# A Trainium2 kernel of four chained residual layers: the odd batch of an adapter moved to the last slot but one, and the split of work around a mixing step changed

## Chip, cores and metric

The kernel runs on one core of one Trainium2 chip. The metric is the time of one execution on the device in microseconds (us). Before the change three runs gave 390.32, 390.70 and 393.04 us, median 390.70.

## What is computed

`x` has 32 batches of 64 rows by 1024 columns, in float32. Four residual layers follow one another; each batch picks its weights by an index:

```python
x = x + einsum('bct,bcd->bdt', x, L0_weights[i0])          # 64x64 mix of the rows, i0 in 0..15
x = x + einsum('bct,bcd->bdt', x, L1_weights[i0])          # a second 64x64 mix, same index
x = x + x @ W.T + 0.5 * (x @ lora_A[i1]) @ lora_B_w.T      # 1024x1024 for all, plus low rank
x = x + x @ L3_weight[i2].T                                # 1024x1024, one of 8 "adapters"
```

The two row mixes act on rows and the two others on columns, so the kernel does the column layers first and mixes rows at the end: for each batch it multiplies a combined 64x64 matrix (layers 0 and 1) with the result of layers 2 and 3.

## The kernel before

**Stage one (to about 186 us)** is layer 2. Products are split in a high and a low part (`fp32r`), three matmuls of 128x128 by 128x512 each, in a scheme with fewer block products (names `P1`, `C11`, `P6`, `C22` and so on). ScalarE (ACT) makes the high part, VectorE (DVE) the low part, SyncE (SP) issues the loads.

DVE also computes a **plan** there, in tiny steps (`plan_steps`, a generator that `take(n)` advances by n pieces): batches of the same adapter are put in pairs, two to a **slot**; an adapter with an odd number of batches has one slot with a single batch. `place` is the position of a batch in this order (twice the adapter's first slot, plus the batch's rank within its adapter). Adapters stand in falling order of their number of slots. Every engine reads the plan's words at run time and branches on them. With these inputs there are 17 slots, 0 to 16. From the counts of matmuls in the trace, slot 4 (the last of the first adapter, of five slots) and slot 16 (the last of all, of an adapter with two slots) hold a single batch.

**Stage two (from about 186 us)** is layer 3, slot by slot. A slot has 8 tiles (k = 0 to 7) of adapter weights. TensorE (PE) does for each tile six matmuls for a pair (`PAIR`, three passes by two halves of 512 columns) or four for a single batch (`ALONE`, two passes by two), line 1469. Written by slot i, the order on PE is (`slot_head`, `slot_tail`):

- tiles 0 to 3 of slot i
- `mix` of slot i-1 (line 1489, four matmuls): the row mix; it needs `r_hi` and `r_lo` of slot i-1
- tiles 4 to 7 of slot i

While PE does the first tiles of slot i, ACT copies the finished rows of slot i-1 as the high part (`rows_hi`, line 750, two instructions), and DVE takes the low part (`rows_lo`, line 1236, two). After `mix`, ACT (`mixed_cols`, line 759) and DVE (`mixed_sum`, line 1247) bring the result to SBUF, and SP stores it. DVE's order in its step i is: `rows_lo` of slot i-1; then, if slot i is the first or the last of an adapter, the low part of four tiles of the next adapter (`adapter_lo`, line 1219); then `mixed_sum` of slot i-1. GpSimd (POOL) makes the low part of the next slot's x (line 467) and the mixing matrices (lines 481 and 483).

**The last slot** is cut by columns (`last_slot`, `columns`): part 0 is columns 0 to 511, part 1 is 512 to 767, part 2 is 768 to 1023, line 1554, all 8 tiles each. Before: part 0, `mix` of the slot ahead (15), part 1, `mix_last` of part 0 (line 1504), six tiles of part 2, `mix_last` of part 1, the other two tiles, six matmuls on no data (line 1308), `mix_last` of part 2. ACT copies each part for `mix_last` to `last_row` (line 815); `last_row` shares memory with the rows of slot 15, which `mix` reads, so this copy waits for `mix`. DVE brings out parts 0 and 1 (line 1282), ACT part 2 (line 831). SP stores slot 15 and then parts 0 and 1 (line 389); ACT issues the store of part 2 (line 833).

Of the kernel before, what the change touches and what calls it, by code (L numbers as in the profile page):

```python
# [13 lines left out]
P = 128  # L14
# [53 lines left out]
def build(nc, xt, indices, w0t, w1, wt, lora_a, lora_b, w3t, plan_c, eye_c, out):  # L68
# [3 lines left out]
    def sb(name, shape, dtype, offset=None):  # L72
        size = 4 * int(np.prod(shape[1:]))
        if offset is None:
            offset = at[0]
            at[0] += (size + 31) // 32 * 32
        return nc.alloc_sbuf_tensor_at(name, shape, dtype, offset=offset)
# [15 lines left out]
    cells = sb("cells", [B, 800], F32)  # L93

    last_mix = sb("last_mix", [P, P], F32, offset=cells_at)
    last_row = sb("last_row", [P, D], F32, offset=aT_at + 4 * KT * CT)
    asked = sb("asked", [B, B], I32)


# [60 lines left out]
    def acc(i):  # L160
        return ps[(1, 3)[i % 2]]
# [7 lines left out]

    def end_acc(p, part):  # L170

        return (acc(p)[:, 0, :], acc(1 - p)[:, 1, 0:256], acc(p)[:, 1, 256:512])[part]

    def end_ps(p, part):

        return (acc(1 - p)[:, 0, :], acc(p)[:, 0, 0:256], acc(1 - p)[:, 1, 0:256])[part]


    events = []
# [22 lines left out]
    def s(name):  # L202
        if name not in sem:
            sem[name] = nc.alloc_semaphore(name)
        return sem[name]
# [64 lines left out]
    def within(eng, value, lo, hi):  # L270
        return nc.s_assert_within(eng.snap(value), lo, hi)
# [5 lines left out]
    with nc.Block() as block:  # L277
# [278 lines left out]
        def _(act):  # L556
# [255 lines left out]
            def last_rows(p, part):  # L812

                act.wait_ge(s("end_left"), part + 1)
                act.activation(last_row[:, END_COLS[part]], end_acc(p, part), ACT.Copy).then_inc(s("end_rows"), 1)

            def last(p):

                act.wait_ge(s("steps"), end_steps)
                act.wait_ge(s("mixed"), end_mixed - 1)  # L820
                rows_hi(1 - p)

                act.wait_ge(s("mixed"), end_mixed)
                last_rows(p, 0)
                act.wait_ge(s(f"stored{1 - p}"), end_stored + 32 * (p - 1))
                mixed_cols(1 - p, ahead)
                last_rows(p, 1)
                last_rows(p, 2)
                act.wait_ge(s(f"stored{p}"), end_stored)
                act.wait_ge(s("end_mixed"), 3)  # L830
                act.activation(stage[:, p, END_COLS[2]], end_ps(p, 2), ACT.Copy).then_inc(s("end_out2"), 1)
                act.wait_ge(s("end_out2"), 1)
                act.dma_start(out_part(end_row, 2), stage[0:T, p, END_COLS[2]]).then_inc(s("end"), 16)

            earlier = None
            for i in range(ENDS):
                earlier, word = step(i, earlier, word)
                if i == LOOK:
                    end_mixed, half, end_word, ahead = end_slot(act, n_slots)
                    odd, end_row = act.snap(end_mixed & 1), batches(end_word)[0]  # L840
                    end_steps = within(act, end_mixed * KT + BEFORE3, KT * ENDS, KT * SLOTS + BEFORE3)
                    end_stored = within(act, half * 32, 32 * (ENDS // 2), 16 * SLOTS)
            with contextlib.ExitStack() as nested:
                for i in range(ENDS, SLOTS - 1):
                    nested.enter_context(act.If(n_slots > i + 1))
                    earlier, word = step(i, earlier, word)
# [7 lines left out]
        def _(dve):  # L854
# [121 lines left out]
            def plan_steps():  # L976
# [23 lines left out]
                def stt(dst, a, k, b, op1, op2):  # L1000
                    after()
                    dve.scalar_tensor_tensor(dst, a, k, b, op1, op2).then_inc(s("chain"), 1)
# [48 lines left out]
                tt(last, first, half, ALU.add)  # L1051
                ts(last, last, -1.0, ALU.add)

                rank, place, wide, places = cell(1), cell(1), cell(B), cell(B)
                stt(row, a, a_own, tri, ALU.is_equal, ALU.mult)
                total(rank, row)
# [1 line left out]
                stt(row[:, 0:NA], e, a_own, first, ALU.is_equal, ALU.mult)  # L1058
                total(place, row[:, 0:NA])
                stt(place, place, 2.0, rank, ALU.mult, ALU.add)  # L1060
                copy(wide, place.to_broadcast([B, B]))
                turned(places, wide)
                yield
# [61 lines left out]
            def take(n=None):  # L1125
                for _ in itertools.islice(making, n):
                    pass
# [63 lines left out]
            t2(1)  # L1191
            x_los(7, stg)
            x_los(8, keep)
            take()
            t4(1)
            x_los(9)
            s1()
# [3 lines left out]
            x_los(11)  # L1201
            x_los(12, stg)
            s4()
            low_parts(2)
            w_los(6, raw_of(w_slot(6)))
            c22(0)
# [95 lines left out]
        def _(pe):  # L1302
# [171 lines left out]

            PAIR, ALONE = ((0, 0), (0, 1), (P, 0)), ((T, 0), (T, 1))

            def slot_part(i, mine, tiles):

                with pe.If(mine[2] < 1):
                    products(i, mine, PAIR, tiles)  # L1480
                with pe.Else():

                    products(i, mine, ALONE, tiles)

            def mix(p, single):

# [39 lines left out]
            def slot_head(i, mine):  # L1526
                if i >= LOOK:
                    next(looking, None)
                slot_ready(i)
                slot_part(i, mine, (0, HALF))  # L1530
                following = slot_record(i + 1) if i < SLOTS - 2 else None
                return following

            def slot_tail(i, earlier, mine):
                if i:
                    pe.wait_ge(s("st"), 4 * i)
                    pe.wait_ge(s("r_lo"), 2 * i)
                    if i > 1:
                        pe.wait_ge(s("staged"), 2 * (i - 1))
                    else:  # L1540
                        pe.wait_ge(s("low_sum"), CH)
                    mix((i - 1) % 2, earlier)
                slot_part(i, mine, (HALF, KT))

            def end_products(p, passes, part, tiles=(0, KT)):

# [13 lines left out]
            def last_slot(p):  # L1560

                def columns(passes):
                    end_products(p, passes, 0)
                    pe.wait_ge(s("st"), end_st)
                    pe.wait_ge(s("r_lo"), end_r_lo)
                    pe.wait_ge(s("staged"), end_r_lo - 2)
                    mix(1 - p, ahead_record[2])

                    end_products(p, passes, 1)
                    mix_last(p, 0)  # L1570
                    end_products(p, passes, 2, (0, END_AT))
                    mix_last(p, 1)
                    end_products(p, passes, 2, (END_AT, KT))


                pe.wait_ge(s("st"), end_st - 4)
                pe.wait_ge(s("r_lo"), end_r_lo - 2)
                pe.wait_ge(s("staged"), end_r_lo - 4)
                mix(p, two_ahead)
                slot_part(3 - p, ahead_record, (HALF, KT))  # L1580
                pe.wait_ge(s("s_lo"), end_r_lo + 4)
                with pe.If(end_record[2] < 1):
                    columns(PAIR)
                with pe.Else():
                    columns(ALONE)
                warm(BRIDGE, acc(1 - p)[:, 1, 256:512])
                mix_last(p, 2)

            pe.wait_ge(s("plan"), 1)
# [51 lines left out]
```

## Time and profile before

| | us |
|---|---|
| median of three runs | 390.70 |
| the profiled execution, as timed | 391.91 |
| its span, first to last instruction | 390.0 |
| PE busy (share) | 378.8 (97%) |
| DVE / ACT / POOL busy | 268.8 / 223.6 / 120.9 |

Times in the profile's rows count from the start of the span. The difference of 1.9 us between the timed execution and its span lies around the span.

### The profile page before, as it was taken

To read this page: it belongs to the slowest core of one execution; us is meant where nothing else is said; L and a number is where in the kernel's file an instruction comes from. 1 tells how busy PE (TensorE), PEld (TensorE's weight loads), DVE (VectorE), ACT (ScalarE), POOL (GpSimd) and SP (SyncE) were. 2 spreads that over 40 slices of the span, in tenths; PEclk is the share of its full clock that TensorE was granted. 3 is DMA by queue.
4 is the path that set the end of the run, shared out by engine and by line. 5 is a ranking of instruction groups with operands and counts; after the bars stand their busy time and mean duration, and the time that the engine had idled before them with its cause. 6 is when DMAs were issued, how large, how long until landed. Compare 5 with 4: busy or idle time off the path is not lost.

```text
span 390.0 us, 7688 instructions
## 1 busy us (share of the span) xinstructions
PE 378.8 (97%) x1760; PEld 314.4 (81%) x1761; DVE 268.8 (69%) x292; ACT 223.6 (57%) x297; POOL 120.9 (31%) x161
## 2 busy tenths in 40 slices
PE   7999999999999999999999999899999999999795
PEld 7888888888888888888888887688888888888574
DVE  3696978856856968456977549952699546899443
ACT  3668658497143784253493449554677357777332
POOL 0000140100003000025864517763258434486300
PEclk9999999999999999999999999999999999999998
DMA  7984904640358485405627224732276322862223
GB/s 245 401 296 163 373 4 134 247 158 4 107 203 289 155 299 196 153 2 216 197 79 217 58 56 145 269 105 58 56 238 202 106 56 57 271 212 63 60 61 86
DMA packets 24187, 61.39 MB, mean 157 GB/s; under 512 B 1906, under 2 KB 2098, under 8 KB 24114
## 3 DMA queue, kind: packets, MB, share of 16 engines
q1 hardware_dynamic: 23792, 60.37, 45.9%
q8 instruction: 30, 0.49, 0.5%
q14 instruction: 43, 0.35, 0.3%
q10 hardware_dynamic: 322, 0.18, 0.2%
HBM read 52.15 MB, written 8.39 MB: 155 GB/s over the span
## 4 chain that ended last, share of the span: by engine, by line
PE 90%; issue 2%; DVE 2%; DMA 1%; DVEq 1%; ACT 1%; POOL 1%; SPq 0%; POOLq 0%; ACTq 0%
PE ps L1469 42%; PE ps L1336 12%; PE ps L1338 12%; PE ps L1337 12%; PE ps L1363 4%; PE ps L1489 4%; PE ps L1554 2%; PE ps L1375 2%; DMA ring_f<-xt 1%; DVE ring L878 1%; DVEq L1146 1%; PE ps L1504 0%; POOL aT L467 0%; ACT ring L568 0%; ACT aT L750 0%
## 5 line engine op out<-in xcount | busy, mean ns | idle before, releaser
L1469 PE MATMUL ps<-ring,aT 128*128 x752 | 173.7, 390 | 0.1
L1469 PEld LDWEIGHTS ps<-ring,aT 128*128 128x128 f32 x752 | 140.9, 188 | 30.3 <-issue 1.2
L1336 PE MATMUL ps<-ring 128*128 128x512 f32 x208 | 81.1, 390 | 0.1
L1337 PE MATMUL ps<-ring 128*128 128x512 f32 x208 | 81.0, 389 | 0.0
L1338 PE MATMUL ps<-ring 128*128 128x512 f32 x208 | 80.9, 389 | 0.0
L467 POOL TENSOR_TENSOR aT<-xT,aT 128x512 fp32r<-128x512 f32 (+1 forms) x36 | 56.4, 1588 | 49.9 <-ACT aT L744 44.6
L1219 DVE TENSOR_TENSOR ring<-raw,ring 128x1024 f32 (+1 forms) x40 | 64.1, 1660 | 5.1 <-ACT ring L730 5.0
L750 ACT ACTIVATE aT<-ps 64x1024 fp32r<-64x1024 f32 x32 | 32.7, 1020 | 48.0 <-PE ps L1469 47.5
L1247 DVE TENSOR_TENSOR stage<-ps,stage 64x1024 f32<-64x1024 f32 x30 | 36.7, 1222 | 31.8 <-ACT stage L759 31.1
L1236 DVE TENSOR_TENSOR aT<-ps,aT 64x1024 fp32r<-64x1024 f32 x32 | 39.1, 1222 | 22.6 <-ACT aT L750 21.9
L1336 PEld LDWEIGHTS ps<-ring 128*128 128x128 f32 x208 | 39.0, 188 | 8.4 <-issue 0.5
L759 ACT ACTIVATE stage<-ps 64x1024 f32<-64x1024 f32 x30 | 30.5, 1017 | 26.5 <-PE ps L1489 26.1
L1338 PEld LDWEIGHTS ps<-ring 128*128 128x128 f32 x208 | 39.0, 188 | 8.2
L1337 PEld LDWEIGHTS ps<-ring 128*128 128x128 f32 x208 | 39.1, 188 | 8.0
L730 ACT ACTIVATE ring<-raw 128x1024 f32 (+1 forms) x40 | 39.5, 1048 | 7.4 <-POOL raw L459 5.0
L617 ACT ACTIVATE xT<-ps 128x512 f32<-128x512 f32 x40 | 22.3, 591 | 19.5 <-PE ps L1338 19.2
L459 POOL TENSOR_TENSOR raw<-raw,eye 128x128 f32<-128x128 f32 x40 | 20.2, 515 | 25.6 <-DMA raw<-w3t 23.6
L878 DVE TENSOR_TENSOR ring<-ring_f,ring 128x1024 fp32r<-128x1024 f32 (+1 forms) x20 | 21.6, 1115 | 7.6 <-ACT ring L568 7.5
L506 POOL TENSOR_TENSOR ring_f<-ring_f,eye 128x128 f32<-128x128 f32 x8 | 5.5, 715 | 65.2 <-DVE ring_f L943 50.7
L744 ACT ACTIVATE aT<-xT 128x512 fp32r (+1 forms) x36 | 19.9, 600 | 3.3 <-DVE xT L954 3.0
L568 ACT ACTIVATE ring<-ring_f 128x1024 fp32r<-128x1024 f32 (+1 forms) x20 | 18.4, 963 | 5.2 <-DVE ring_f L912 3.1
L1489 PE MATMUL ps<-aT,st 128*128 128x512 f32 x64 | 17.6, 396 | 3.7 <-POOL st L483 2.2
(93 smaller groups left out, 330.2 us busy)
## 6 DMA issues: line engine op xcount, KB each, us to landing
raw<-w3t SPq DMA_DIRECT2D x40, 512.0 KB, 4.3
ring_f<-xt SPq DMA_DIRECT2D x8, 1024.0 KB, 8.4
raw<-xt SPq DMA_DIRECT2D x8, 1024.0 KB, 5.0
out<-stage SPq DMA_DIRECT2D x30, 256.0 KB, 3.2
ring_f<-wt SPq DMA_DIRECT2D x4, 1024.0 KB, 7.3
xT<-xt SPq DMA_DIRECT2D x3, 1024.0 KB, 10.9
xT<-wt SPq DMA_DIRECT2D x2, 1024.0 KB, 15.8
ring_f<-wt SPq DMA_DIRECT2D x4, 256.0 KB, 5.9
```

The costliest lines, as they stand in the source:

```text
L467: pool.tensor_tensor(x3_split(i, ks, P + h * T, T), xT[:, ks, bass.ds(which[h] * T, T)], as_f32(x3_split(i, ks, h * T, T)), ALU.subtract). ...
L730: act.activation(dst, adapter_raw(t), ACT.Copy).then_inc(s("w_hi"), 1)
L750: act.activation(r_tile(h)[own, :], acc(p)[own, :, :].rearrange("p a n -> p (a n)"), ACT.Copy)\
L759: act.activation(stage[own, p, :], mixed_ps[h][other, :, :].rearrange("p a n -> p (a n)"), ACT.Copy)\
L1219: dve.tensor_tensor(in_two(unit_of(t, 1)), adapter_raw(t), as_f32(in_two(unit_of(t, 0))), ALU.subtract)\
L1236: dve.tensor_tensor(r_tile(h)[other, :], acc(p)[own, :, :].rearrange("p a n -> p (a n)"), as_f32(r_tile(h)[own, :]), ALU.subtract).then_in ...
L1247: dve.tensor_tensor(dst, mixed_ps[h][own, :, :].rearrange("p a n -> p (a n)"), dst, ALU.add)\
L1336: pe.matmul(dst, hi_of(qw)[:, k, cs], hi_of(qx)[:, k, :], start=start and k == 0, stop=False, skip_group_check=True)
L1337: pe.matmul(dst, hi_of(qw)[:, k, cs], lo_of(qx)[:, k, :], start=False, stop=False, skip_group_check=True)
L1338: last = pe.matmul(dst, lo_of(qw)[:, k, cs], hi_of(qx)[:, k, :], start=False, stop=stop and k == HALF - 1, skip_group_check=True)
L1469: last = pe.matmul(acc(i)[:, n, :], x3_split(i, k, start, P), ring[:, bass.ds(off + (part * D + n * 512), 512)], start=(k == 0 and j == 0) ...
L1489: last = pe.matmul(dst[:, n, :], st[:, p, h, :], r_tile(h)[:, 512 * n:512 * (n + 1)], start=start, stop=stop)
```

## The change

Five edits:

1. **Plan.** Three more cells: `moved` marks adapters with at least three slots; for one with an odd count it becomes the rank 2·half-3, else a rank that no batch reaches. Batches from this rank on are placed one position later. The single batch thus takes the last slot but one, and the last two batches are a pair. For the first adapter (nine batches, five slots) slot 3 now holds the single batch and slot 4 a pair. The adapter of slots 15 and 16 has only two slots and stays as it is.
2. **Tiles ahead of mixing.** A single batch's slot does five tiles ahead of `mix` and three behind, a pair's four and four as before.
3. **Place of the plan's steps on DVE.** What was one run of steps (`take()`) is now six pieces (`take(6)`) there and the rest behind `s4()`.
4. **The last slot.** Parts 0 and 1 now stand ahead of `mix` of slot 15. The accumulators and result places of part 1 and 2 are exchanged to fit.
5. **`last_row`** lies in `raw`, the adapters' load buffer, so ACT copies parts 0 and 1 ahead of the wait for `mix`; it waits for `w_lo` of the last adapter's tiles first.

```diff
-    last_row = sb("last_row", [P, D], F32, offset=aT_at + 4 * KT * CT)
+    last_row = raw[:, 0, :]
...
-        return (acc(p)[:, 0, :], acc(1 - p)[:, 1, 0:256], acc(p)[:, 1, 256:512])[part]
+        return (acc(p)[:, 0, :], acc(p)[:, 1, 0:256], acc(1 - p)[:, 1, 256:512])[part]
...
-        return (acc(1 - p)[:, 0, :], acc(p)[:, 0, 0:256], acc(1 - p)[:, 1, 0:256])[part]
+        return (acc(1 - p)[:, 0, :], acc(p)[:, 0, 0:256], acc(p)[:, 1, 0:256])[part]
...
+                act.wait_ge(s("w_lo"), end_adapter)
+                last_rows(p, 0)
+                last_rows(p, 1)
                 act.wait_ge(s("mixed"), end_mixed)
-                last_rows(p, 0)
                 act.wait_ge(s(f"stored{1 - p}"), end_stored + 32 * (p - 1))
                 mixed_cols(1 - p, ahead)
-                last_rows(p, 1)
                 last_rows(p, 2)
...
+                moved, odd, start = cell(NA), cell(NA), cell(1)
+                ts(moved, half, 3.0, ALU.is_ge)
+                stt(odd, half, 2.0, cnt, ALU.mult, ALU.subtract)
+                tt(odd, odd, moved, ALU.mult)
+                ts(moved, half, 2.0, ALU.mult, float(2 * B - 3), ALU.add)
+                stt(moved, odd, float(-2 * B), moved, ALU.mult, ALU.add)
+                yield
...
+                stt(row[:, 0:NA], e, a_own, moved, ALU.is_equal, ALU.mult)
+                total(start, row[:, 0:NA])
+                ts(rank, rank, start, ALU.is_ge, place, ALU.add)
+                copy(place, rank)
...
             x_los(8, keep)
-            take()
+            take(6)
             t4(1)
...
             s4()
+            take()
             low_parts(2)
...
-            def slot_part(i, mine, tiles):
+            def slot_part(i, mine, second):
+                def tiles(front):
+                    return (front, KT) if second else (0, front)
                 with pe.If(mine[2] < 1):
-                    products(i, mine, PAIR, tiles)
+                    products(i, mine, PAIR, tiles(HALF))
                 with pe.Else():
-                    products(i, mine, ALONE, tiles)
+                    products(i, mine, ALONE, tiles(HALF + 1))
...
                     end_products(p, passes, 0)
+                    end_products(p, passes, 1)
                     pe.wait_ge(s("st"), end_st)
                     pe.wait_ge(s("r_lo"), end_r_lo)
                     pe.wait_ge(s("staged"), end_r_lo - 2)
                     mix(1 - p, ahead_record[2])
-                    end_products(p, passes, 1)
                     mix_last(p, 0)
```

How it moves instructions. First DVE in stage one, between the low parts of `x_los(8)` (the first row) and those of `t4(1)` and `s1()`. Before, the plan's tail and its end stand here (line 1122 writes the last word; 912 is `t4`, 943 is `s1`):

```order
L1002 SCALAR_TENSOR_TENSOR cells<-cells 32x1 x6
L998 TENSOR_SCALAR cells<-cells 32x3 x3
L1010 CAST cells<-cells 32x3
...
L1122 CAST plan<-cells 1x1
L912 TENSOR_TENSOR ring_f<-ring_f,raw 128x2048
L878 TENSOR_TENSOR ring<-ring_f,ring 128x1024 x2
L943 TENSOR_TENSOR ring_f<-ring_f,raw 128x2048
```

Of the change, the same place and the end of `s4` (line 951) with `low_sum` (965):

```order
L1004 SCALAR_TENSOR_TENSOR cells<-cells 32x1 x6
L914 TENSOR_TENSOR ring_f<-ring_f,raw 128x2048
L880 TENSOR_TENSOR ring<-ring_f,ring 128x1024 x2
L945 TENSOR_TENSOR ring_f<-ring_f,raw 128x2048
...
L951 TENSOR_TENSOR ring_f<-ring_f,raw 128x2048
L1000 TENSOR_SCALAR cells<-cells 32x3 x3
...
L1137 CAST plan<-cells 1x1
L965 TENSOR_TENSOR low<-ps,low 128x512
```

The tail of the plan has left its place ahead of `t4(1)` and now stands between `s4` and `low_sum`.

Second, ACT in the last slot. Before (750 is `rows_hi` of slot 15, 759 or 763 `mixed_cols`, 815 the copies of the parts, 831 the result of part 2):

```order
L750 ACTIVATE aT<-ps 64x1024 x2
L815 ACTIVATE last_row<-ps 128x512
...
L759 ACTIVATE stage<-ps 64x1024 x2
...
L815 ACTIVATE last_row<-ps 128x256 x2
L831 ACTIVATE stage<-ps 128x256
```

Of the change:

```order
L750 ACTIVATE aT<-ps 64x1024 x2
L815 ACTIVATE raw<-ps 128x512
L815 ACTIVATE raw<-ps 128x256
...
L759 ACTIVATE stage<-ps 64x1024 x2
...
L815 ACTIVATE raw<-ps 128x256
L832 ACTIVATE stage<-ps 128x256
```

The copy of part 1 has moved ahead of `mixed_cols`. Third, PE in the last slot, single batch; the rows just before and behind `mix`, before:

```order
L1554 MATMUL ps<-ring,aT 128x512
L1493 COMPARE_AND_BRANCH
L1489 MATMUL ps<-aT,st 128x512 x4
...
L1554 MATMUL ps<-ring,aT 128x256
L1504 MATMUL ps<-last_row,last_mix 128x512
```

Of the change:

```order
L1573 MATMUL ps<-ring,aT 128x256
L1512 COMPARE_AND_BRANCH
L1508 MATMUL ps<-aT,st 128x512 x4
...
L1523 MATMUL ps<-raw,last_mix 128x512
L1573 ISA
```

`mix` now follows the 256-column matmuls of part 1, and `mix_last` of part 0 follows `mix` at once.

## Rows read from the trace of the kernel before

**Rows 1.** PE's waits, whole span: waited for, us in total, times, longest.

```profile
PE ps L1489 <- POOL st L483: 2.2, 1, 2.2
PE ps L1489 <- issue: 1.5, 3, 1.1
```

**Rows 2.** Chain of waits, slots 3 to 5: start us, us, what.

```profile
224.78 0.91 PE ps L1489 x4
225.68 9.07 PE ps L1469 x40
...
234.92 1.19 PE ps L1489 x4
...
258.88 0.91 PE ps L1489 x4
```

**Rows 3.** Timeline of DVE around slot 4: start us, us, what, [idle before].

```profile
232.21 2.48 DVE L1236 TENSOR_TENSOR aT<-ps,aT 64x1024 fp32r<-64x1024 f32 x2 [2.75 <-ACT aT L750]
235.53 5.74 DVE L1219 TENSOR_TENSOR ring<-raw,ring 128x1024 f32 x4 [0.84 <-ACT ring L730]
...
243.81 2.48 DVE L1236 TENSOR_TENSOR aT<-ps,aT 64x1024 fp32r<-64x1024 f32 x2
```

**Rows 4.** Timeline of POOL: the x of slot 4.

```profile
222.33 2.54 POOL L467 TENSOR_TENSOR aT<-xT,aT 128x512 fp32r<-128x512 f32 x2 [3.83 <-ACT aT L744]
```

**Rows 5.** Chain of waits, last slot.

```profile
373.96 3.63 PE ps L1554 x16
...
377.83 1.18 PE ps L1489 x4
379.02 1.90 PE ps L1554 x16
```

**Rows 6.** Timeline of all engines, last slot.

```profile
375.13 2.48 DVE L1236 TENSOR_TENSOR aT<-ps,aT 64x1024 fp32r<-64x1024 f32 x2 [2.71 <-ACT aT L750]
...
383.23 1.02 DVE L1282 COPY stage<-ps 128x512 f32<-128x512 f32 x2
...
385.40 0.47 SPq L389 DMA_DIRECT2D out<-stage  x1
...
386.08 0.58 ACTq L833 DMA_DIRECT2D out<-stage  x1
```

**Rows 7.** DMA issues, 383 to 390 us: count, KB each, us to landing.

```profile
out<-stage SPq DMA_DIRECT2D x2, 256.0 KB, 3.9
out<-stage SPq DMA_DIRECT2D x1, 192.0 KB, 2.9
out<-stage ACTq DMA_DIRECT2D x1, 64.0 KB, 3.5
```

**Rows 8.** Timeline of DVE, 104 to 140 us: the plan's tail, `t4`, `s1`, `s4`, `low_sum`.

```profile
104.34 0.60 DVE L998 TENSOR_SCALAR cells<-cells 32x3 f32<-32x3 f32 x3
...
107.98 2.29 DVE L912 TENSOR_TENSOR ring_f<-ring_f,raw 128x2048 f32<-128x2048 f32 x1
...
118.07 2.29 DVE L943 TENSOR_TENSOR ring_f<-ring_f,raw 128x2048 f32<-128x2048 f32 x1 [4.18 <-DMA ring_f<-wt]
...
134.88 2.28 DVE L949 TENSOR_TENSOR ring_f<-ring_f,raw 128x2048 f32<-128x2048 f32 x1
139.96 0.69 DVE L963 TENSOR_TENSOR low<-ps,low 128x512 f32<-128x512 f32 x1 [2.80 <-ACT low L605]
```

**Rows 9.** Timeline of all engines: low rank's high part, and the matmul that needs it.

```profile
140.68 2.18 ACT L610 ACTIVATE low_split<-low 64x256 fp32r<-64x256 f32 x5 [0.76 <-DVE low L963]
...
143.23 0.39 PE L1375 MATMUL ps<-low_split,b_split 128*128 128x512 f32 x1
```

**Rows 10.** Timeline of all engines, 358 to 368 us: ahead of `mix` of slot 14.

```profile
360.05 0.23 POOL L483 CAST st<-aT 64x64 fp32r x1 [0.17 <-POOL st L481]
...
361.91 2.48 DVE L1236 TENSOR_TENSOR aT<-ps,aT 64x1024 fp32r<-64x1024 f32 x2
...
367.18 1.18 PE L1489 MATMUL ps<-aT,st 128*128 128x512 f32 x4 [2.21 <-POOL st L483]
```

More of the change, by code:

```diff
@@ L842, in _ @@
                     end_stored = within(act, half * 32, 32 * (ENDS // 2), 16 * SLOTS)
+                    end_adapter = within(act, get(end_word, THIS) * KT + WBASE, WBASE, WBASE + NA * KT)
             with contextlib.ExitStack() as nested:
@@ L1529, in slot_head @@
                 slot_ready(i)
-                slot_part(i, mine, (0, HALF))
+                slot_part(i, mine, False)
                 following = slot_record(i + 1) if i < SLOTS - 2 else None
@@ L1542, in slot_tail @@
                     mix((i - 1) % 2, earlier)
-                slot_part(i, mine, (HALF, KT))
+                slot_part(i, mine, True)
             def end_products(p, passes, part, tiles=(0, KT)):
@@ L1579, in last_slot @@
                 mix(p, two_ahead)
-                slot_part(3 - p, ahead_record, (HALF, KT))
+                slot_part(3 - p, ahead_record, True)
                 pe.wait_ge(s("s_lo"), end_r_lo + 4)
@@ L1585, in last_slot @@
                     columns(ALONE)
-                warm(BRIDGE, acc(1 - p)[:, 1, 256:512])
+                warm(BRIDGE, acc(p)[:, 1, 256:512])
                 mix_last(p, 2)
```

## The prediction

> **What bounds the kernel now.** I read first the list of PE's waits, because the engine table shows PE nearly always busy and every other engine far less. PE has few waits, and nearly all of them stand just ahead of a `mix` (line 1489): one of 2.2 us put down to POOL, and three of 1.5 us together, the longest 1.1 [rows 1]. So a change can win only what lies in these, in the start of PE behind them, and in the stores behind PE's end. I then read the chain of waits around slot 4, the first single batch [rows 2]. Forty matmuls take 9.07 us, 0.227 us each. From the start of `mix` of slot 2 (224.78) to that of slot 5 (258.88) are 34.10 us. The work in it is three mixes of 0.91 us and 128 matmuls (24 + 16, 16 + 24, 48) of 0.227, so 2.73 + 29.02 = 31.75. **2.35 us are lost around this one single batch.**
>
> The timeline of DVE says why. `rows_lo` of slot 3 runs 232.21 to 234.69, and `mix` of slot 3 starts at 234.92, 0.23 later: a single batch's four tiles (16 x 0.227 = 3.63 us) ahead of mixing are shorter than the way through ACT and DVE. Slot 3 ends 24 matmuls after 224.78 + 0.91, at 231.1; DVE's low part is there 3.6 us later and the mix 3.8. Behind it DVE has the adapter's last-slot work, four tiles of 5.74 us from 235.53, then `mixed_sum`, and only at 243.81 `rows_lo` of slot 4, until 246.29 [rows 3]. Slot 4 was over at about 239.8, since it is single, and PE waited 1.1 us for that [rows 1]. So short a slot and DVE's largest load fall together.
>
> **The change, part by part.**
>
> *Plan (single batch in slot 3) and five tiles ahead.* The count of matmuls stays. Slot 2 ends 24 matmuls ahead of 224.78, at 219.3. Now 20 matmuls follow (4.54 us), so PE is ready to mix slot 2 at 223.9; the rows need 3.8 us, 223.1: no wait, 0.7 us to spare. Then 12 matmuls of slot 3, 24 of slot 4: `mix` of slot 3 is due 5.45 us after slot 3's end: 1.6 us to spare, if DVE is free, and it is, for slot 3 is neither first nor last of its adapter. In slot 4, DVE starts the four tiles when `rows_lo` of slot 3 is over, about 231; with 5.74 us for them and about 2.5 or less for `mixed_sum` it is free at about 239, when the slot (a pair now) ends. `rows_lo` of slot 4 is over by about 243, and PE mixes at 244.7. That is the pattern of the other adapters, whose last slots are pairs, and none of them has a wait in [rows 1]. The x of slot 4 is made by POOL from 222.33 to 224.87 and slot 4 starts at about 227.5 [rows 4]. I take the whole 2.35 us; the lower bound is 1.7, if the starts of PE behind a single batch stay slow.
>
> *Last slot.* Before, part 0 starts at 373.96 with 3.63 us of work, and part 1 at 379.02 [rows 5]: 5.06 us for 3.63 + 0.91, **0.52 us lost**, since `rows_lo` of slot 15 ends only at 375.13 + 2.48 = 377.61 [rows 6]. With part 1's 1.90 us ahead of `mix` as well, PE comes there at 379.49, so nothing is left of it. PE's end falls by 0.52. But `mix` of slot 15 now starts at 379.49 instead of 377.83, 1.66 later. ACT used to copy part 0 (0.6 us) between `mix` and `mixed_cols`; that is done ahead now, so `mixed_cols`, `mixed_sum`, DVE's copies and SP's stores come some 0.8 us later. DVE's copies began at 383.23; they were not last. SP's last issue goes from 385.40 to 386.2, landing 2.9 us later at 389.1; ACT's goes from 386.08 to 385.56, landing after 3.5 us at 389.1, where it was 389.6 [rows 6, 7]. Both queues end together, and I take 0.4 us of the 0.52. If SP's last store needs the 3.9 us of the stores of 256 KB [rows 7], it lands at 390.1, a loss of 0.5.
>
> *`last_row` in `raw`.* Same copies, same shapes; the added wait on `w_lo` is for tiles that DVE finished before slot 15. Behind it on ACT wait only these copies. Zero.
>
> *The plan's steps.* The tail behind `s4` is 104.34 to 107.98, 3.64 us; four instructions more stand in the piece ahead of it. `t4(1)` comes about 1.8 us earlier (3.64 less some 1.8 for pieces that came later) [rows 8]. Behind `s4` the tail stands ahead of `low_sum`. With `s4` over at 137.16 (134.88 + 2.28) it would end at 140.8, and `low_sum` starts at 139.96 [rows 8]: 0.84 us late. That matters: ACT's high part ends at 142.86 and PE uses it at 143.23 [rows 9], so about 0.4 us are spare, and PE would lose 0.5 to 0.8. But `s1` waits 4.18 us for a load of W that SP issues only behind `t4(1)` [rows 8]. With `t4(1)` earlier by 1.8 us this load, `s1`, the copies behind it and `s4` come earlier by as much, 135.3, and the tail ends at 139.0, before 139.96. I take zero; the bounds are zero and 0.8.
>
> *Code.* A pair's slot jumps over a single batch's code of five tiles instead of four in its first half, three instead of four in the second. The nearest row is the jump out of slot 15 to the last slot: `mix` of slot 14 starts 2.21 us after PE was through, though its mixing matrix was done at 360.28 and its rows at 364.39. The name POOL in [rows 10] is thus not the cause; no wait of the program is left but the branches over the code of slots that do not exist. A jump can cost this much. Yet in slot 4 PE jumped over 24 matmuls of a pair's half slot and no wait inside line 1469 stands in [rows 1]; 20 matmuls are a shorter way. Zero. The Trainium skill ("Runtime: NRT & Kernel Launch", Instruction fetch mechanics) says that a taken branch to a target outside the present two blocks of instructions forces a fetch before work goes on. This trace agrees with its 2.21 us. By that rule a change of code length alone can put another jump across a block's edge; one such would leave 2.75 - 2.21 = 0.5 us of the sum.
>
> **Sum.** 2.35 + 0.4 = 2.75 us. The profiled execution would take 391.91 - 2.75 = 389.2; it stood 1.2 us above the median of 390.70, so the median becomes **387.9 us**.
>
> **Rivals.**
>
> - *The tail of the plan is not absorbed* (chance 0.11). The load of W also waits for PE to finish with its buffer; if that is later than `t4(1)`, `s4` stays. Loss of 0.8: 388.7. Against: before, SP issued right behind `t4(1)`.
> - *The stores take the last slot's gain back* (0.15): 2.35 less 0.5: 388.8. For: both queues end within 0.1 us in my sum.
> - *The plan's move does nothing or DVE still comes late* (0.06): 0.4 us alone: 390.3. Against: the move changes the only load that coincides.
> - *The jump to the last slot becomes short* by the new code positions (0.05): 2.21 us more: 385.7.
> - *More jumps miss* (0.06): the longer way over a single batch's code is not fetched in time in the fifteen pair slots of the loop. Price 2.21 us each less what PE has queued. It decides from two misses on: 390.7 - 2.75 + 4.42 = 392.4, slower than before; from four, 396.8, clearly slower; all fifteen give 421. Against it speaks the longer jump in slot 4. The rule of the Trainium skill named above is the one that would bring this.
>
> The forecast itself has 0.57.
>
> **Chances and range.** Below 1% (3.9 us) a measurement of this kernel hardly tells a difference. Forecast, the first three rivals and two misses lie within it; faster by over 1% needs the short jump and runs that fall low, 0.12; slower 0.05; within 1% 0.83. The range takes in the first two rivals, 388.8, most of the third, and the spread of the runs before (390.32 to 390.70, one at 393.04), on both sides: 386.6 to 390.4.
>
> **What would show it.** No wait ahead of the mixes of slots 2, 3 and 4; 36 matmuls between the mixes of slots 2 and 3 instead of 40, and from the mix of slot 2 to that of slot 5 132 of them, so 2.73 + 29.93 = 32.7 us (the mix of slot 2 itself comes four matmuls earlier). `mix` of the last slot directly behind part 1, no wait; SP's and ACT's last landings within half a microsecond. PE's stage one without a new wait at the low-rank matmuls, DVE's `t4(1)` near 106.2. The 2.21 us ahead of slot 14's mix unchanged. I would be wrong if PE shows waits inside line 1469 or at 143 us, or if the stores end later than 389.6 less 2.35.

## The result

Over 22 runs of each kernel on one chip the changed kernel took 391.0 us in the median (388.98 to 392.5), the kernel before 392.93 (390.32 to 395.76). The ratio is 0.9952 [0.9931, 0.9973]: faster by 1.9 us, where 2.75 were forecast, and a time of 391.0 where 387.9 were forecast. Two things stand behind that. The three runs known beforehand (median 390.70) were low ones: of the 3.1 us between forecast and result, 2.2 are the starting point. The other 0.9 is the sum, and in it one term, the last slot, had its mechanism wrong, as told below.

### The profile after

The profiled execution took 392.04 us, its span 390.2. That is no less than the 391.91 of the one before, though the median fell: TensorE's clock was lowered for a while in it, which cost 1.5 us (last section). Top of the page: busy time of the engines, and TensorE's granted clock in 40 slices.

```profile
PE 379.6 (97%) x1760; PEld 316.6 (81%) x1761; DVE 269.7 (69%) x301; ACT 223.4 (57%) x297; POOL 121.6 (31%) x161
...
PEclk9999999999999999999999999999999999999897
```

PE's waits of the changed kernel, whole span: waited for, us in total, times, longest.

```profile
PE ps L1508 <- POOL st L483: 2.0, 1, 2.0
PE ps L1324 <- POOL st L448: 1.4, 1, 1.4
PE ps L1379 <- DVE a_sel L1176: 0.4, 1, 0.4
```

The three waits ahead of a `mix` (now line 1508) put down to "issue", 1.5 us in [rows 1], are gone. The one put down to POOL stands, 2.0 against 2.2. The chain of waits around the single batch, now in slot 3 (start us, us, what), answers [rows 2]:

```profile
223.35 0.91 PE ps L1508 x4
224.26 8.30 PE ps L1485 x36
232.56 0.91 PE ps L1508 x4
233.46 10.88 PE ps L1485 x48
244.34 0.91 PE ps L1508 x4
...
256.13 0.91 PE ps L1508 x4
```

PE works without a gap: from the mix of slot 2 to that of slot 5 are 32.78 us of work, where 34.10 were [rows 2], although the stretch now holds four matmuls (0.91 us) more: a gain of 2.23 us for equal work. The plan's edit did what it was to do. Now the timeline of the last slot (start us, us, what, [idle before]), which answers [rows 5, 6]:

```profile
372.32 5.70 PE L1573 MATMUL ps<-ring,aT 128*128 x32
...
377.86 1.09 PE L1508 MATMUL ps<-aT,st 128*128 128x512 f32 x4
...
379.29 2.06 ACT L759 ACTIVATE stage<-ps 64x1024 f32<-64x1024 f32 x2 [0.84 <-PE ps L1508]
...
380.34 2.47 DVE L1263 TENSOR_TENSOR stage<-ps,stage 64x1024 f32<-64x1024 f32 x2 [4.21 <-ACT stage L759]
...
382.71 0.67 PE L1523 MATMUL ps<-raw,last_mix 128*128 128x256 f32 x2
382.85 1.02 DVE L1298 COPY stage<-ps 128x512 f32<-128x512 f32 x2
...
384.11 0.59 ACTq L834 DMA_DIRECT2D out<-stage  x1
385.75 0.47 SPq L389 DMA_DIRECT2D out<-stage  x1
```

The slot begins at 372.32; before, it began at 373.80 by the same view. PE has no wait in it, and its last matmul ends at 383.38 instead of 385.34: 11.1 us after the slot's start instead of 11.5. But the span ends 17.9 us after the slot's start, where it was 16.2. **The last slot became 1.7 us longer, although PE leaves it 0.5 us earlier.** ACT's small store goes out 0.5 us earlier after the slot's start than before (11.79 us against 12.28); SP's last store goes out 1.8 us later (13.43 against 11.60, [rows 6]). And it needs longer to land. DMA issues of the last 10 us, count, KB each, us to landing, against [rows 7]:

```profile
out<-stage SPq DMA_DIRECT2D x2, 256.0 KB, 3.5
out<-stage SPq DMA_DIRECT2D x1, 192.0 KB, 4.0
out<-stage ACTq DMA_DIRECT2D x1, 64.0 KB, 2.4
```

The 192 KB took 4.0 us, where they took 2.9; they are now what ends the kernel, while before it was the 64 KB of ACT (12.28 + 3.5 against 11.60 + 2.9).

### The profile page after: what moved, and what is told of

It reads as the page before. It is cut to its first block, busy times and chain, and to the rows that moved or that the text cites. A ratio compares the mean times of both kernels' runs of the same rounds, so it can differ in the third digit from the quotient of the medians.

```text
span 390.2 us, 7701 instructions
## 1 busy us (share of the span) xinstructions
PE 379.6 (97%) x1760; PEld 316.6 (81%) x1761; DVE 269.7 (69%) x301; ACT 223.4 (57%) x297; POOL 121.6 (31%) x161
## 4 chain that ended last, share of the span: by engine, by line
PE 89%; DVE 3%; issue 2%; DVEq 1%; DMA 1%; ACT 1%; POOL 1%; SPq 0%; POOLq 0%; ACTq 0%
PE ps L1485 43%; PE ps L1353 12%; PE ps L1352 12%; PE ps L1354 12%; PE ps L1379 4%; PE ps L1508 4%; PE ps L1391 2%; PE ps L1573 1%; DMA ring_f<-xt 1%; DVE ring L880 1%; DVEq L1161 1%; POOL aT L467 0%; DVEq L277 0%; ACT ring L568 0%; DVE stage L1263 0%
## 5 line engine op out<-in xcount | busy, mean ns | idle before, releaser
L750 ACT ACTIVATE aT<-ps 64x1024 fp32r<-64x1024 f32 x32 | 32.7, 1023 | 49.8 <-PE ps L1485 49.4
L506 POOL TENSOR_TENSOR xT<-xT,eye 128x128 f32<-128x128 f32 x4 | 5.8, 1482 | 46.0 <-DVE xT L939 46.0
```

Source lines behind the costliest of these rows:

```text
L750: act.activation(r_tile(h)[own, :], acc(p)[own, :, :].rearrange("p a n -> p (a n)"), ACT.Copy)\
```

## The experiments

Ratios are to the kernel before, run on the same chip, with a 95% interval. There are twelve runs of each kernel where nothing else is said. They came in three groups, each on a chip of its own with the kernel before beside it (medians 393.05, 393.24 and 392.95 us), so kernels of different groups are compared by their ratios. "Last slot" is the time from its first product to the end of the span, in the profile.

### Parts of the change

**The changed kernel once more** (nothing edited), for its spread.

> The changed kernel once more, beside its parts. Theory (three terms): the move of the single batch and the five tiles give 2.3 us, seen in the trace as mixes of slots 2 to 5 without a wait; the last slot's new order brings PE's end 0.5 forward but the end of the stores little or nothing; stage one is even. So 2.3 to 2.8 us below the kernel before, less what a lowered clock costs in a run. Rival: the last slot's order costs what the trace's end shows (its SP store lands 389.75 against 389.6), and only 1.0 to 2.0 us are left.

392.04 us (389.08 to 394.51), ratio 0.9977 [0.9948, 1.0007]. Last slot 18.0 us and 4.0 us of landing again, so the 17.9 are no accident of one execution. The interval includes 1: by these runs alone the change is not shown to be faster.

**The plan's move and five tiles, without the edit of the last slot.** The first keeps the plan's tail ahead of `t4(1)`, the second has it behind `s4` as the change does.

```diff
-                    end_products(p, passes, 1)
                     pe.wait_ge(s("st"), end_st)
...
+                    end_products(p, passes, 1)
                     mix_last(p, 0)
```

(with ACT's `last_rows`, `last_row` and the PSUM areas as before), and in the first also

```diff
-            take(6)
+            take()
             t4(1)
...
             s4()
-            take()
             low_parts(2)
```

> The single batch in the last slot but one and five tiles ahead; the last slot and last_row as before, and the plan's steps in one run as before (with the added steps in it, so t4(1) comes some 1.8 us later than in the kernel before). If the tail's place is of no weight for stage one: 2.3 us below the kernel before. If the later load of W delays PE in stage one: 0.5 to 1.8 us of this are lost, seen as a wait of PE between 120 and 150 us.

> As m1, but with the plan's tail behind s4, as in the change. Theory: 2.3 us below the kernel before, whatever the last slot's order does. If the last slot's order is a loss, this is faster than the changed kernel by that loss; if a gain of 0.4, slower by it.

With the tail ahead of `t4(1)`: 391.88 us, ratio 0.997 [0.994, 0.9999]. With the tail behind `s4`: 390.15, ratio 0.993 [0.9904, 0.9956], 1.7 us (0.4%) below it. Both have a last slot of 16.2 to 16.3 us. Both ran beside the changed kernel of the paragraph above, and the second was 1.9 us faster than that (390.15 against 392.04): this is what the last slot's edit costs there, and it fits the 1.7 us of the profile. DVE in stage one of the first (timeline):

```profile
109.29 2.29 DVE L913 TENSOR_TENSOR ring_f<-ring_f,raw 128x2048 f32<-128x2048 f32 x1
...
119.35 2.29 DVE L944 TENSOR_TENSOR ring_f<-ring_f,raw 128x2048 f32<-128x2048 f32 x1 [4.15 <-DMA ring_f<-wt]
```

and two of PE's waits there:

```profile
PE ps L1350 <- DVE ring L879: 0.9, 1, 0.9
...
PE ps L1377 <- DVE ring L879: 0.4, 1, 0.4
```

The longer plan puts `t4` at 109.29 where it stood at 107.98 [rows 8], and PE loses 0.9 + 0.4 us for DVE's copies. So the instructions added to the plan are free only because its tail was moved behind `s4`: the split buys back what they would have cost. And the second kernel is the measure for the rest: without the last slot's edit the change gives 0.7%, 2.75 us.

**The last slot's edit alone**, on the kernel before: the same lines as above, the other way round.

> Only the last slot's order and last_row in raw; plan and tiles as before. My forecast's step: 0.4 us below the kernel before (0.52 on PE). Rival: the stores end it: SP's last store lands as late as before or later, 0 to 0.5 us above the kernel before, while PE's end still comes 0.5 earlier.

394.02 us, ratio 1.0029 [0.9996, 1.0063]; last slot 18.6 us: SP's last store goes out 13.66 us after the slot's start and needs 4.5 to land. It does not gain the forecast 0.1% (0.4 us), which lies outside the interval; its point estimate is a loss of 1.1 us, and the interval just takes in no change at all.

**Five tiles alone**, the single batch left in slot 4.

```diff
-                stt(moved, odd, float(-2 * B), moved, ALU.mult, ALU.add)
+                ts(moved, moved, float(2 * B), ALU.add)
```

> As m2 (last slot as before, plan's steps split), with five tiles ahead of mixing, but the single batch stays in the last slot of its adapter (slot 4). Theory: five tiles take away the small wait ahead of the mix of slot 3 (0.3 to 0.4 us of the 2.35) and lengthen nothing; the wait of 1.1 us and more ahead of the mix of slot 4 stays, since DVE's four tiles set it. So about 1.9 us slower than m2, near the kernel before. Rival: the tiles are the larger part, and it is within 1 us of m2.

392.59 us, ratio 0.9992 [0.9965, 1.0018]: nothing. PE's timeline, mixes of slots 2 to 5:

```profile
224.17 1.07 PE L1507 MATMUL ps<-aT,st 128*128 128x512 f32 x4
...
235.05 1.07 PE L1507 MATMUL ps<-aT,st 128*128 128x512 f32 x4
...
246.22 1.19 PE L1507 MATMUL ps<-aT,st 128*128 128x512 f32 x4 [1.64 <-issue]
...
258.71 1.07 PE L1507 MATMUL ps<-aT,st 128*128 128x512 f32 x4
```

The wait ahead of the mix of slot 3 is gone, the one ahead of the next mix has grown from 1.1 to 1.64, and mix 2 to mix 5 takes 34.54 us. What bound PE here was DVE's four tiles together with the short slot; the tile more ahead of mixing only changes where one waits for it.

**The move alone**, four tiles ahead, on the kernel with the plan's edits only.

```diff
-                    products(i, mine, ALONE, tiles(HALF + 1))
+                    products(i, mine, ALONE, tiles(HALF))
```

> As m2 (last slot as before), but with four tiles ahead of mixing for a single batch too: the move alone. Theory: only the small wait ahead of the mix of the slot before the single one comes back (0.3 to 0.4 us), so 0.4 slower than m2 and 1.9 faster than the kernel before. Rival: move and tiles need each other, and it is near the kernel before.

391.17 us, ratio 0.9957 [0.9928, 0.9986]. In the profile PE waits 0.17 us ahead of the mix of slot 2, and none stands ahead of the mixes of slots 3 and 4, but the 40 matmuls behind that wait take 9.45 us where 40 took 9.07 before [rows 2]. From stage two's first product to the mix of slot 5 it is 72.46 us (183.76 to 256.22), with five tiles 71.79 (184.56 to 256.35): the tile is worth 0.7 us in these profiles, more than the wait alone. The move is most of the gain. The ratios of the two lie 0.27% apart, within their intervals.

### The last slot

**The 192 KB of the last slot stored by ACT** instead of SP, behind its own 64 KB, so that they don't stand behind slot 15's two stores.

```diff
-                sp.wait_ge(s("end_out"), 2)
-                store_cols(0, front, "end")
                 with sp.If(single < 1):
+                    sp.wait_ge(s("end_out"), 2)
                     store_cols(1, front, "end_pair")
...
+                act.dma_start(out[bass.ds(end_row, 1), :, front].rearrange("a t d -> (a t) d"),
+                              stage[0:T, p, front]).then_inc(s("end"), 16)
```

> The changed kernel, but the store of parts 0 and 1 of a single last batch is issued by ACT, behind its store of part 2, not by SP. In the changed kernel SP's second store of slot 15 holds SP for 1.2 us instead of 0.5, at the time of ACT's issue, and SP's last store is issued 1.9 us behind the end of DVE's copies and lands 4.0 us later, last of all. Theory A (the order of issue on SP costs most of it): ACT issues it about 0.6 us behind its first, near 1 us earlier than SP did; the end comes 0.5 to 1 us earlier than in the changed kernel. Theory B (the bytes in flight set the landing: 0.75 MB in 3 us): it lands no earlier, and the time is that of the changed kernel within 0.3 us.

391.18 us, ratio 0.9949 [0.9922, 0.9976]; last slot 16.75 us. The store goes out 12.55 us after the slot's start instead of 13.43 and lands after 3.7. The profile shows 1.2 us gained, but no gain shows in the runs: the change itself had 0.9952 and 0.9977.

**Only two of part 1's eight tiles ahead of `mix`**, ACT's copy of it back behind `mixed_cols`.

```diff
-                    end_products(p, passes, 1)
+                    end_products(p, passes, 1, (0, 2))
                     pe.wait_ge(s("st"), end_st)
...
+                    end_products(p, passes, 1, (2, KT))
                     mix_last(p, 0)
```

> The changed kernel, but only two of part 1's eight tiles stand ahead of the mix of slot 15 (four matmuls, about 0.5 us, the length of the wait that stood there), the other six behind it, and ACT copies part 1 behind mixed_cols. If the late mix of slot 15 is what makes the changed last slot longer (17.7 us from its first product to the span's end against 16.0 before), this takes 15.6 to 16.1 and the kernel is 1.5 to 2 us faster than the changed one. If the extra copies or the memory of last_row cost it, it stays at 17 or more.

390.4 us, ratio 0.9936 [0.9905, 0.9968]; last slot 16.15. Its timeline:

```profile
374.98 1.19 PE L1508 MATMUL ps<-aT,st 128*128 128x512 f32 x4
...
376.50 2.06 ACT L759 ACTIVATE stage<-ps 64x1024 f32<-64x1024 f32 x2 [1.17 <-PE ps L1508]
...
377.55 2.48 DVE L1263 TENSOR_TENSOR stage<-ps,stage 64x1024 f32<-64x1024 f32 x2 [2.90 <-ACT stage L759]
...
382.24 0.48 SPq L389 DMA_DIRECT2D out<-stage  x1
382.75 0.58 ACTq L834 DMA_DIRECT2D out<-stage  x1
```

`mixed_cols` starts 5.65 us after the slot's start (370.85), where the change has 6.97 and the kernel before 5.88. SP's last store goes out after 11.39 us. PE has no wait here either, and its last matmul ends 11.2 us after the slot's start. So most of PE's 0.5 us can be had, but the end does not follow (16.15 against 16.2 before): it hangs on the stores.

**Slot 15's two stores left out**, the output of its two batches not written, all else as in the change.

```diff
-                store(1 - p, ahead, "end_ahead")
                 store_last(p, end_rows, get(end_word, SINGLE))
...
-            sp.wait_ge(s("end_ahead"), 32)
```

> The changed kernel without SP's two stores of slot 15 (these two batches of the output are left out). In the changed kernel SP's last store is issued 1.9 us behind the end of DVE's copies and lands 4.0 us later, after everything else. If the two stores ahead of it, which now overlap ACT's, are the cause: it is issued 0.3 us behind the copies, lands within 3 us, and the end comes 2 us earlier or more (bounded then by ACT's store). If it is DVE's late copies alone, only the issue moves and 1 us or less is won.

387.95 us (four runs), ratio 0.9883 [0.9823, 0.9942]; last slot 15.1. SP's last store goes out as soon as its data is there, and lands after 2.9 us:

```profile
out<-stage SPq DMA_DIRECT2D x1, 192.0 KB, 2.9
out<-stage ACTq DMA_DIRECT2D x1, 64.0 KB, 2.7
```

DVE's copies start 10.5 us after the slot's start here as in the change (381.72 - 371.19; 382.85 - 372.32), so the compute is the same. The 2.8 us between 15.1 and 17.9 are what goes with slot 15's stores: 1.6 us by which SP issues the last one earlier (11.87 us against 13.43) and 1.1 us of landing. The two parts have different causes.

How the issues stand on SP tells the first part. SP's timeline at the end, before:

```profile
383.66 1.30 SPq L379 DMA_DIRECT2D out<-stage  x2
385.40 0.47 SPq L389 DMA_DIRECT2D out<-stage  x1
```

and of the change, over the last 8 us:

```profile
383.28 2.03 SPq L379 DMA_DIRECT2D out<-stage  x2
385.75 0.47 SPq L389 DMA_DIRECT2D out<-stage  x1
```

The two stores of slot 15 take SP 1.30 us before and 2.03 in the change, because the second (from 384.10) took 1.21 us instead of 0.47. ACT issues its own DMA at 384.11, 0.01 us behind its start. The same stretch is 1.30 with two tiles of part 1 ahead, where ACT issues after SP is through, and 1.82 and 2.17 in the two other kernels in which ACT's issue falls into it (the ACT store above, and the one without the far jump below). Five kernels agree, but none moves ACT's issue alone: this is a reading of timelines, not shown by an edit. And ACT is not the only thing that goes with a long issue. Of SP's stores of earlier slots, which ACT never issues beside, some 40 in the fourteen profiles took 0.7 to 1.5 us too, as here in the change (one took 1.41 of the 2.21):

```profile
320.31 2.21 SPq L379 DMA_DIRECT2D out<-stage  x2
```

The second part, the landing, can be read from the packets of the DMA queues, which the trace keeps one by one. SP's stores go through q1, ACT's through q10; q8 is of the kind "instruction", by its name the loading of code. Of the change, the packets begun from 387.5 to 388.6 us (queue, kind: packets, MB, share of 16 engines), then the stretch from 388.00 to 388.50 (its last two columns are DMA share and GB/s), then the packets begun from 388.5 to 389.4:

```profile
q1 hardware_dynamic: 43, 0.09, 28.6%
q8 instruction: 1, 0.02, 5.7%
...
388.00:388.50 0.50, 0.00 (x0) 0.00 (x0) 0.00 (x0) 0.00 (x0) 0.00 (x0) 0.50 0.00 0
...
q1 hardware_dynamic: 5, 0.01, 5.7%
```

By 387.98, 75 of the 80 packets of the 192 KB are over. The last five, one sixteenth of the store, begin at 388.52, just when a packet of 16 KB of code that began at 387.52 is over, and end at 389.31, 1.3 us behind the others. The two other profiles with a long landing show the same: there the code's packets end at 386.48 and 392.44, and the last five of the store begin at 386.48 and 392.43. In the kernel without slot 15's stores the store's packets are over at 385.31 and the code's begins at 385.74. In the kernel without the far jump (below), whose last store is issued as late and has the same stores ahead of it, they are over at 384.28, the code's begins at 384.45, and the store lands after 2.5 us. The kernel before is not free of it: its packet of code ran from 386.53 to 387.49, while slot 15's stores were under way, and the last packets of ACT's 64 KB ended at 389.13, the others at 388.29. So the long landing goes with a load of code that gets in the way of one sixteenth of the last store, and not with the bytes in flight. No edit moves that load alone; this too is a reading.

### The wait that the profile puts down to POOL

**Without PE's code for slots that do not exist here** (more than 17 slots); for this input the computation is the same.

```diff
             with contextlib.ExitStack() as nested:
-                for i in range(ENDS - 1, SLOTS - 2):
+                for i in range(ENDS - 1, ENDS):
                     nested.enter_context(pe.If(n_slots > i + 2))
```

> The changed kernel without PE's code for slots that would exist only with more than 17 slots (it computes the same here, since there are 17). If the wait of 2.0 to 2.6 us ahead of the mix of slot 14 is the jump over that code, it goes, and 2 us are won; if it is a late engine or a late semaphore (the profile puts it down to POOL), it stays.

387.1 us (six runs, 386.85 to 389.52), ratio 0.9858 [0.9818, 0.9897]. PE around the mix of slot 14, timeline:

```profile
358.69 3.33 PE L1485 MATMUL ps<-ring,aT 128*128 x14
361.86 1.16 PE L1508 MATMUL ps<-aT,st 128*128 128x512 f32 x4
```

No wait, where it was 2.21 us [rows 10] and 2.0 in the change, with POOL's work unchanged. The last slot is 16.7 us here (landing 2.5), 1.2 shorter than in the change. The cause of that wait is shown: it is PE's branch over that code.

**The last slot's code at each place where the slots can end**, so that the jump over code that is not run is short (on the kernel with two tiles of part 1 ahead).

```diff
                 for i in range(ENDS - 1, SLOTS - 2):
-                    nested.enter_context(pe.If(n_slots > i + 2))
+                    with pe.If(n_slots < i + 3):
+                        last_slot((i + 1) % 2)
+                    nested.enter_context(pe.Else())
```

> h1 (two tiles of part 1 ahead of the mix of slot 15), and PE's code laid out anew for any number of slots: the code of the last slot stands directly at each place where the slots can end, ahead of the next slot's, not once behind all of them. With 17 slots PE jumps over one last slot's code ahead of slot 14's second half, and then needs no jump to its own. If a jump's cost goes by its length, the wait of 2.1 us ahead of the mix of slot 14 goes and at most a part of it comes back one slot earlier: 1 to 2.2 us below h1. If any jump out of the code ahead costs 2 us, the wait only moves to the mix of slot 13 and the time is h1's.

394.03 us, ratio 1.0026 [0.9996, 1.0056]. I expected a gain; it lost all that the kernel with two tiles ahead had won (0.9936). PE's waits:

```profile
PE ps L1485 <- issue: 2.2, 1, 2.2
PE ps L1508 <- issue: 2.1, 1, 2.1
```

There are now two such waits, each as long as the one was: ahead of the mix of slot 13 (352.27), where PE passes over one last slot's code, and ahead of the products behind that mix (355.61). The first is what I had expected if a short jump costs as much as a long one. Between the mix and the products no slot's code is passed, only the short branches between a pair and a single batch; why a second wait stands there stays open. So the price did not fall with the way that a jump goes, and the layout of the code cost a second wait, by a rule that these runs do not show.

**Both**: two tiles of part 1 ahead, and no code for further slots.

> h1 without PE's code for more than 17 slots. If both findings add up: the gain of j1 and that of h1 over the changed kernel together, 385.1 less 0.5 to 1.3 us in the trace's span (last slot in 16.1 us from its first product instead of j1's 16.7), 383.8 to 384.6, some 6 us below the kernel before. If the last slot's gain was tied to the wait ahead of it, it stays at 385.

386.46 us (six runs, 385.73 to 386.84), ratio 0.9835 [0.9793, 0.9878], last slot 15.7 us: the fastest version, which holds only for inputs with at most 17 slots. Of those that hold for all, the two at 0.993 and 0.9936 are ahead of the change by point estimate.

## Why the prediction was right and wrong

**The starting point.** I took the 1.2 us between the profiled execution and the median of three runs off the sum. With 22 runs the median is 392.93, 1.0 above the profiled execution and not 1.2 below. A kernel whose three runs lie 2.7 us apart does not give a median to within 1 us, and the range should have had that on its upper side.

**Plan and five tiles, 2.35 us: right.** The mix of slot 2 comes at 223.35 (forecast 223.9), that of slot 4 at 244.34 (244.7), mix 2 to mix 5 takes 32.78 (32.7). The half microsecond by which the first comes early is none of the change's: stage two began 0.5 us sooner (184.20 against 184.72), and a profile of the same kernel run again has it at 183.58. Without the last slot's edit the kernel gains 0.7%, 2.75 us [1.7, 3.8], which holds the 2.35. Neither edit gives it alone: the move does most, the fifth tile without the move nothing.

**The plan's steps, zero: right, for the reason given.** With the tail left in its place PE lost 0.9 + 0.4 us, and the runs 1.7. DVE in stage one of the change (timeline), against [rows 8]:

```profile
106.24 2.29 DVE L914 TENSOR_TENSOR ring_f<-ring_f,raw 128x2048 f32<-128x2048 f32 x1
...
116.44 2.29 DVE L945 TENSOR_TENSOR ring_f<-ring_f,raw 128x2048 f32<-128x2048 f32 x1 [4.29 <-DMA ring_f<-wt]
...
133.33 2.28 DVE L951 TENSOR_TENSOR ring_f<-ring_f,raw 128x2048 f32<-128x2048 f32 x1
...
139.07 0.14 DVE L1137 CAST plan<-cells 1x1 int32<-1x1 f32 x1
139.44 0.69 DVE L965 TENSOR_TENSOR low<-ps,low 128x512 f32<-128x512 f32 x1 [0.23 <-ACT low L605]
```

`t4(1)` at 106.24 (forecast 106.2), the load of W and `s1` earlier with it, `s4` over at 135.61 (135.3), the tail at 139.21 (139.0), and `low_sum` still waits for ACT. The margin is 0.23 us: it was a close call.

**The last slot, a gain of 0.4 us: wrong. It is the step that failed.** The PE half of it held (no wait, PE out 0.5 us earlier), and ACT's store went out where I said, 11.79 us after the slot's start (11.76). The words that failed are "`mixed_cols`, `mixed_sum`, DVE's copies and SP's stores come some 0.8 us later" and "landing 2.9 us later". `mixed_cols` came 1.09 us later after the slot's start: `mix` moved by 1.5 us, and the copy done ahead gave back only 0.4. The 0.8 was also a slip of its own terms, for 1.66 less 0.6 is 1.06. SP's second store then took 0.7 us longer to issue, which the sum held at its old length, so SP's last store went out 1.8 us later. And the 192 KB took 4.0 us to land, where the sum had 2.9. Forecast for the store's landing is 12.4 + 2.9 = 15.3 us after the slot's start; it was 13.43 + 4.0 = 17.4. The pessimistic bound, 3.9 us by the stores of 256 KB and a loss of 0.5, came near the landing by luck: the bytes are not what made it long (2.5 us with the same stores in the kernel without the far jump), and the late issue was missing from it. With a loss of 1.7 the profile's sum is 2.35 - 1.7 = 0.65 us. The runs gave 1.9 [1.1, 2.7] in the first measurement and 0.9 [-0.3, 2.0] when the changed kernel was run again; in that group, where the kernel without the last slot's edit stood beside it, the edit cost 1.9 us. So the second measurement agrees with the profile's sum, and why the first came out better stays open. The rival "the stores take the last slot's gain back" had 0.15 and named the right place, SP's last store landing last. That its total, 1.9 us, is the measured one is luck: its loss was 0.5, and the last slot lost 1.7.

**The jump: right.** No wait inside the slots was added, and the one ahead of slot 14's mix stood, 2.0 us. Reading it as a branch and not as POOL was right. The rule of the Trainium skill ("Runtime: NRT & Kernel Launch", Instruction fetch mechanics), that a taken branch leaving the two present blocks has to be fetched for, agrees with the runs that leave the code out: without it no wait. The kernel with the last slot's code laid out anew shows that it takes more than this rule to say how many such waits a layout has.

## What to carry to other kernels

In the last stage count the way to the last byte, not the busiest engine's: an edit that let PE finish 0.5 us earlier made the last slot 1.7 us longer, since it delayed the mix that three stores in a queue waited for. Look at the packets, too, when one landing is long: here five packets of eighty stood behind a load of code. Where a short slot and the load of another engine fall together, move one of the two; more work ahead of the wait only hands the wait on to the next slot. A wait of some 2 us whose named releaser was done long before is worth a look at the branches: leaving out code that this input never runs gave more (another 1%) than the change did, for inputs that never need it.

## What the runs showed of the chip

The wait at PE's branch over unused code was 1.7 to 3.0 us in the eleven profiles with one such wait, and 2.2 and 2.1 in the one with two. In the two kernels without that code it was gone. TensorE's clock after that wait differed from one execution to the next. A stretch of 2 us behind the wait: us, PE, PEld, DVE, ACT and POOL busy (instructions), granted clock, DMA share, GB/s; of the change, first profile:

```profile
366.00:368.00 2.00, 2.00 (x6) 1.61 (x5) 0.92 (x1) 1.95 (x2) 0.12 (x1) 0.50 0.01 4
```

and of the same kernel, run again:

```profile
366.00:368.00 2.00, 2.00 (x10) 1.66 (x9) 1.78 (x2) 1.18 (x2) 0.33 (x1) 1.00 0.03 8
```

At 0.50 (1.2 GHz) PE did six matmuls in 2 us, else ten; from the mix to the last slot's start it took 8.1 us (364.23 to 372.32), in the kernel with two tiles of part 1 ahead, at full clock, 6.6 (364.25 to 370.85). So the drop cost 1.5 us. It stands in 5 of the 12 profiles with such a wait, and in neither of the two without. The times fit: with the wait twelve or more runs of a kernel spread over 3.3 to 5.5 us, without it six runs over 2.7 and 1.1 (fewer runs, so a narrower spread by that alone). That is as much as the whole change moved. Leaving out the branch gained 3.7 and 4.0 us, by the ratios. Of that the wait is 2.0 and 2.1 in the profiles and the shorter last slot 1.2 and 0.5; the lowered clock, gone too, can be the rest, but no run separates it.

SP's issue of a store, 0.47 us as a rule, took 1.0 to 1.4 us in all five profiles in which ACT's DMA issue began 0.01 us behind it, 1.21 in the change; but issues of 0.7 to 1.5 us stand elsewhere without ACT, so what makes one long is not settled. The last slot's 192 KB took 4.0, 4.0 and 4.5 us to land in the three profiles that have the last slot's edit with nothing taken back, and 2.8 or 2.9 in nine others, that without slot 15's stores among them. The kernel without the far jump has that edit too, and there it took 2.5, after the same late issue. In the three long ones five of the store's 80 packets began only when a 16 KB packet of code was over, 1.3 to 1.8 us behind the rest.
